# Experts by choice: rows gathered five tiles ahead instead of four, and the late partial sums fetched in one row

## The chip, the cores and the metric

One core of a Trainium2 chip. The metric is the device time of one execution in microseconds; for the kernel before it is the median of three runs. All stages of the model run in one launch on this core.

## The reference

A graph attention layer with a feed-forward block comes first; the change touches only the last stage, a mixture of experts over 4096 rows of 512 values.

```python
K = 2; EPS = 1e-06; B, S, D, F, E = (8, 256, 512, 256, 8)   # here 4096 rows
logits = xf @ router_w
gate_vals, idx = jax.lax.top_k(logits, K)
gates = jax.nn.softmax(gate_vals, axis=-1)
out = jnp.zeros_like(xf)
for e in range(E):
    h = jax.nn.relu(xf @ w1[e] + b1[e]) @ w2[e] + b2[e]
    y = _layernorm(xf + h, gamma[e], beta[e])
    w = jnp.sum(jnp.where(idx == e, gates, 0.0), axis=-1)
    out = out + w[:, None] * y
```

The result is added to x, and xf is the layer norm of x. Both x and its norm stand side by side in one table in memory.

## The kernel before, in words

The function `experts` first loads all rows once to compute the router's logits, picks each row's two experts, and sorts the rows into tiles of 128 rows that share an expert. Every row occurs once by its first choice and once by its second. For each choice there are EACH = 39 tiles (32 full ones and up to 7 that are not full), so a loop runs over SLOTS = 78 slots. Slots 0 to 38 are the first half (first choices), slots 39 to 77 the second (second choices).

A row of the table `z3` (called t_z in the profile) has WITH_SUM = 1028 values of 4 bytes in two parts of PART = 514: the sum so far, and the normalised row with its two gates. In the first half a slot gathers whole rows of `z3` by an indirect DMA, computes its expert, adds gate times result to the sum part, and scatters the whole rows to the table `summed` (t_summed). In the second half a slot gathers whole rows of `summed` and scatters its result to `out`. So whole rows of the second half can be gathered only when all scatters of the first half have landed. For the first LATE_PARTS slots of the second half (`late(n)`, here slots 39 to 43) this is split: the normalised part comes from `z3` in the gather's turn, and the sum part comes from `summed` later, by `late_part(n)`, with a semaphore of its own, `moved_part`.

All of these DMAs are issued by GpSimd (POOL), in this order and each after its own waits:

```python
for n in range(LEAD):
    gather(n)
for n in range(SLOTS):
    if n + LEAD < SLOTS:
        gather(n + LEAD)
    if n:
        scatter(n - 1)
    if late(n):
        late_part(n)
```

`gather(m)` (L1989 for a late slot's part, L1995 for whole rows) fills ring buffer m modulo TURN = 8; it waits until slot m-8 is done (`e_done`) and, where that was a slot of the first half, until its scatter has landed (`wait_put`). `scatter(n)` (L2015 in the first half, L2012 in the second) waits for `e_done` of slot n. `late_part(n)` (L2005) waits by `all_put` for the landing of the last four scatters of the first half.

In iteration n the other engines do the following, in this order.

- TensorE (PE): `turn_rows(n + 2)` transposes the gathered rows (L2274, after `wait_rows`), then it reads the number of slot n+1's expert from memory into a register (`expert`), then `up(n + 1)` (L2332), `down_bias(n)` (L2346), `down(n)` (L2351) and `turn_hidden(n + 1)` (L2340).
- ScalarE (ACT): `columns(n + 2)` copies the transposed rows (L2059), `hidden(n + 1)` (L2064), `hidden_columns(n + 1)` (L2070), the root of slot n's variance (L2099), which waits for VectorE, and `outer(n + 1)` (L2076).
- VectorE (DVE): `spread(n)` adds the row (L2220; its start is used below as the clock of the loop) and takes the statistics (L2222, L2224), `outer(n - 1)` ends the slot before (L2246, signals `e_done`), then `gain(n)` and `add_base(n)` (L2230). For a late slot `add_base(n)` stands after `gain(n)` and first waits for `moved_part` of that slot.

Of the kernel before, what the change touches and what calls it, by code (L numbers as in the profile page):

```python
# [25 lines left out]
VROW = HEADS * VHEAD  # L26
PART = C + 2
WITH_SUM = 2 * PART
LATE_PARTS = 5
BOTH = C + VROW  # L30
MERGED = (3, 11, 19, 27)
DVE_HEADS = (HEADS - 1, HEADS - 2)
# [1759 lines left out]
def experts(nc, moved, moved_part, count, z3, router, w1, b1, w2, b2, gamma, beta, summed, b2_home, out):  # L1792
# [10 lines left out]
    KC = C // P  # L1803
    T = NODES // P
    E, _, F = w1.shape
    FC = F // P
    TOP = 2
    EACH = T + E - 1
    SLOTS = TOP * EACH
    TURN = 8  # L1810
    LEAD = 4
    Y = 4
    HALF = 4
    LIST_TURNS = 4
# [2 lines left out]
    with ExitStack() as ctx:  # L1817
        def sb(name, shape, dt=F32):
            return ctx.enter_context(nc.sbuf_tensor("m_" + name, shape, dt))

        def ps(name, shape, dt=F32):
            return ctx.enter_context(nc.psum_tensor("m_" + name, shape, dt))
# [56 lines left out]
        put_at = sb("put_at", [P, SLOTS], I32)  # L1879
        part_of = sb("part_of", [P, 2, LATE_PARTS], I32)  # L1880
        turned = [ps(f"turned{b}", [P, C]) for b in range(2)]
# [41 lines left out]
        def second(n):  # L1923
            return n >= EACH

        def late(n):
            return EACH <= n < EACH + LATE_PARTS

# [3 lines left out]
        def wait_put(eng, n):  # L1932
            eng.wait_ge(put[n % Y], count + 16 * (n // Y + 1))
# [5 lines left out]
        @block.sync  # L1939
        def _(eng):  # L1940
            eng.dma_start(router_sb[:, :, :], router.rearrange("(k p) e -> p k e", p=P)).then_inc(s_c, 16)
            eng.dma_start(b2_rows[:, :], b2).then_inc(s_b2_rows, 16)
            z_of = z3[:, PART:PART + C]
            for i in range(T // TURN):
                for u in range(TURN):
                    if i:
                        r_turn.wait(eng, i - 1, u)
                    eng.dma_start(z_rows[:, u, :], tile_rows(z_of, i, TURN, u)).then_inc(r_load.sem(u), 16)
            eng.wait_ge(s_b2_cut, 3 * PARTS - 4)
            eng.dma_start(b2_home, b2_parts[:, :, :]).then_inc(s_b2_home, 16)  # L1950
            eng.dma_start(b1_sb[:, :, :], b1).then_inc(s_w1, 16)
            eng.dma_start(w1_sb[:, :, :, :], w1.rearrange("e (k p) f -> p e k f", p=P)).then_inc(s_w1, 16)
            eng.dma_start(w2_sb[:, :, :, :], w2.rearrange("e (k p) c -> p e k c", p=P)).then_inc(s_w2, 16)
            eng.wait_ge(s_b2_home, 16)
            eng.dma_start(b2_sb[:, :, :], b2_home.rearrange("e k c -> k e c")).then_inc(s_b2, 16)
            for dst, a, landed in ((gamma_sb, gamma, s_gamma), (beta_sb, beta, s_beta)):
                eng.dma_start(flat(dst[:, :, :]), a.rearrange("e c -> (e c)").partition_broadcast(P)).then_inc(landed, 16)

        @block.gpsimd
        def _(eng):  # L1960
            for a, value in ((ones, 1.0), (zeros, 0.0), (eps, EPS), (ones_b, 1.0)):
                eng.memset(a[:, :], value).then_inc(s_cut, 1)
            eng.memset(go_on[:, :, :], 1.0).then_inc(s_cut, 1)
            eng.memset(go_on_e[:, :, :], 1.0).then_inc(s_cut, 1)
            for a, step, n, down, first_one in ((falling, -1, E, 0, E), (row_id, 0, 1, 1, 1), (slot_at, 1, EACH, 0, 0),
                                                (turn_b, 1, T, 0, 0)):
                eng.iota(a[:, :], pattern=[[step, n]], base=first_one, channel_multiplier=down,
                         allow_small_or_imprecise_dtypes=True).then_inc(s_cut, 1)
            eng.iota(iota_2[:, :, :], pattern=[[1, P], [0, 2]], base=0, channel_multiplier=0,
                     allow_small_or_imprecise_dtypes=True).then_inc(s_cut, 1)  # L1970
            eng.wait_ge(s_cut, 11)
            eng.memset(go_on[:, :, 0:1], 0.0).then_inc(s_cut, 1)
            eng.memset(go_on_e[:, :, 0:1], 0.0).then_inc(s_cut, 1)
            for m, of, op, other in ((ident, ones, ALU.is_equal, 0.0), (not_after, zeros, ALU.is_gt, -1.0)):
                eng.affine_select(out=m[:, :], in_=of[:, :], compare_op=op, fill=other, base=0,
                                  pattern=[[1, P]], channel_multiplier=-1).then_inc(s_cut, 1)

            z3_parts, summed_parts = (a.rearrange("n (h w) -> (n h) w", h=2) for a in (z3, summed))

            def gather(n):  # L1980
                u = n % TURN
                if n >= TURN:
                    e_done.wait(eng, 0, n - TURN)
                    if not second(n - TURN):
                        wait_put(eng, n - TURN)
                if late(n):
                    if n == EACH:
                        eng.wait_ge(s_ready, 2)
                    eng.indirect_dma_start(rows_sb[:, u, PART:], None, z3_parts,  # L1989
                                           bass.IndirectOffsetOnAxis(part_of[:, 1, n - EACH:n - EACH + 1], 0)  # L1990
                                           ).then_inc(got[u], 16)
                else:
                    if second(n):
                        all_put(n)
                    eng.indirect_dma_start(rows_sb[:, u, :], None, summed if second(n) else z3,  # L1995
                                           bass.IndirectOffsetOnAxis(row_of[:, n:n + 1], 0)).then_inc(got[u], 16)

            def all_put(n):
                if n <= EACH + LATE_PARTS:
                    for k in range(EACH - Y, EACH):  # L2000
                        wait_put(eng, k)

            def late_part(n):
                all_put(n)
                eng.indirect_dma_start(rows_sb[:, n % TURN, 0:PART], None, summed_parts,  # L2005
                                       bass.IndirectOffsetOnAxis(part_of[:, 0, n - EACH:n - EACH + 1], 0)
                                       ).then_inc(moved_part[n - EACH], 16)

            def scatter(n):
                e_done.wait(eng, 0, n)  # L2010
                if second(n):
                    eng.indirect_dma_start(out, bass.IndirectOffsetOnAxis(put_at[:, n:n + 1], 0), y[:, n % Y, :], None,  # L2012
                                           bounds_check=NODES - 1, oob_is_err=False).then_inc(put[n % Y], 16)
                else:
                    eng.indirect_dma_start(summed, bass.IndirectOffsetOnAxis(put_at[:, n:n + 1], 0), rows_sb[:, n % TURN, :], None,  # L2015
                                           bounds_check=NODES - 1, oob_is_err=False).then_inc(put[n % Y], 16)

            eng.wait_ge(s_ready, 1)
            eng.wait_ge(s_gate_home, 16)
# [4 lines that stand above are left out]
                    gather(n + LEAD)  # L2024
                if n:
                    scatter(n - 1)
                if late(n):
                    late_part(n)
            scatter(SLOTS - 1)
            for n in range(SLOTS - Y, SLOTS):  # L2030
                wait_put(eng, n)
# [72 lines left out]
        def _(eng):  # L2104
# [69 lines left out]
            for c in range(TOP):  # L2174
# [33 lines left out]
                if c == 1:  # L2208
                    few = token[:, c, 0:LATE_PARTS]
                    st.link(nc.vector.tensor_scalar(part_of[:, 0, :], few, 2.0, None, ALU.mult))  # L2210
# [167 lines left out]
def graph_layer(nc, a, out):  # L2378
# [5 lines left out]
    with ExitStack() as ctx:  # L2384
        moved = [ctx.enter_context(nc.semaphore(f"moved{n}")) for n in range(MOVES)]
        moved_both = [ctx.enter_context(nc.semaphore(f"moved_both{n}")) for n in range(2)]
        moved_part = [ctx.enter_context(nc.semaphore(f"moved_part{n}")) for n in range(LATE_PARTS)]
        stages(nc, a, out, moved, moved_both, moved_part, scratch)
# [58 lines left out]
```

## Time and profile before

| | |
|---|---|
| median of three runs | 3304.93 us (3302.91 to 3306.12) |
| profiled execution, its own time | 3307.92 us |
| span of its profile | 3306.2 us |
| PE, PEld, DVE, ACT, POOL busy | 2772.7, 1710.6, 2521.6, 1701.4, 1935.0 us |
| mean granted clock | 0.93 of full speed |
| the 78 slots in that span | from about 2868 to 3297 us |

The span is the time between the first and the last instruction that the profiler saw; the execution's own time is 1.7 us longer. The busy shares are those of the whole program; the loop over the slots is its last eighth and has limits of its own.

### The profile page before, as it was taken

The page shows a single profiled execution, that of the slowest core. Times are in us where ns is not written, and L with a number is a line of the kernel's source. Part 1 is how long each engine was busy: PE and PEld are TensorE (multiplying, and loading weights), DVE is VectorE, ACT ScalarE, POOL GpSimd, SP SyncE. Part 2 cuts the span into 40 slices and gives each one's busy share as a digit, 9 for nine tenths or more (in the row PEclk, how much of TensorE's full clock was granted, in tenths as well). Part 3 has the DMA queues.
Part 4 walks back from the last instruction along what each step waited for, and adds up shares of the span by engine and source line. Part 5 has one row for each costly group of instructions (what it writes and reads, how often), then busy time and mean ns, then how long its engine had stood idle before and what let it go on. Part 6 is the DMA issues. An engine that isn't in the chain of part 4 may idle for free. (4 is left out here: it accounts for less than half of the span.)

```text
span 3306.2 us, 51862 instructions
## 1 busy us (share of the span) xinstructions
PE 2772.7 (84%) x12057; PEld 1710.6 (52%) x12057; DVE 2521.6 (76%) x5238; ACT 1701.4 (51%) x5713; POOL 1935.0 (59%) x1959
## 2 busy tenths in 40 slices
PE   6987888780888888886999999998999997699797
PEld 6544444450333333332555655567888885355454
DVE  8776666660999999998999999996566563577576
ACT  5222222220666566555999999993443432244343
POOL 2777777776777777776777777762222221044344
PEclk9888888885999999998999999997999999899999
DMA  4554555544888888887777878774221222765343
GB/s 168 197 182 167 173 173 170 174 147 152 261 258 261 262 260 259 261 258 243 216 231 231 233 231 232 230 205 112 68 71 61 74 71 94 226 200 188 119 155 108
DMA packets 248065, 610.11 MB, mean 185 GB/s; under 512 B 60466, under 2 KB 69578, under 8 KB 243037
## 3 DMA queue, kind: packets, MB, share of 16 engines
q0 software_dynamic: 130000, 376.49, 38.2%
q1 hardware_dynamic: 113661, 230.27, 20.2%
q8 instruction: 113, 1.85, 0.2%
q14 instruction: 179, 1.47, 0.1%
q10 hardware_dynamic: 4112, 0.03, 0.1%
HBM read 488.89 MB, written 123.26 MB: 185 GB/s over the span
## 5 line engine op out<-in xcount | busy, mean ns | idle before, releaser
L1275 PE MATMUL at_pair<-wide,hot_t 128*128 x1152 | 583.2, 621 | 120.7 <-ACT hot_t L1126 106.4
L1324 PE MATMUL at_pair<-product,v_hot 128*128 128x260 f32 x2304 | 617.2, 400 | 48.7 <-DVE product L1074 21.2
L364 POOL DMA_INDIRECT records<-staged,address x544 | 545.6, 1003 | 182.5 <-issue 161.9
L914 POOL DMA_INDIRECT fetched<-t_v,at_index x504 | 487.3, 967 | 188.0 <-issue 86.6
L904 POOL DMA_INDIRECT fetched<-t_k,at_index x504 | 487.4, 967 | 154.8 <-issue 102.0
L1324 PEld LDWEIGHTS at_pair<-product,v_hot 128*128 128x128 f32 x2304 | 394.5, 190 | 266.2 <-issue 158.4
L660 PE MATMUL qkv_prod<-wide 128*128 128x512 f32 x768 | 397.5, 681 | 96.8 <-ACT wide L404 96.8
L1066 DVE TENSOR_TENSOR wide<-at_pair,wide 128x520 f32 x576 | 397.3, 690 | 14.1 <-issue 10.3
L1275 PEld LDWEIGHTS at_pair<-wide,hot_t 128*128 128x128 f32 x1152 | 186.2, 189 | 385.0 <-issue 381.8
L1134 ACT ACTIVATE product<-product 128x64 f32<-128x64 f32 x864 | 215.9, 250 | 286.3 <-DVE product L993 284.9
L993 DVE TENSOR_TENSOR product<-at_pair,fetched 128x512 f32<-128x512 f32 x504 | 342.3, 682 | 25.3 <-DMA fetched<-t_k,at_index 18.9
L947 DVE TENSOR_REDUCE raw_score<-product 128x7 f32<-128x448 f32 x576 | 329.7, 575 | 0.0
L660 PEld LDWEIGHTS qkv_prod<-wide 128*128 128x128 f32 x768 | 165.6, 220 | 304.5 <-issue 205.6
L1213 ACT ACTIVATE product<-fetched,act_weight 128x65 f32<-128x65 f32 x1008 | 288.8, 333 | 0.0
L1074 DVE TENSOR_TENSOR product<-fetched,at_turn 128x390 f32<-128x390 f32 x504 | 276.4, 549 | 2.7 <-ACT act_weight L1193 1.5
L1526 POOL TENSOR_TENSOR f_base<-f_base,wide 128x512 f32<-128x512 f32 x32 | 41.0, 1280 | 343.6 <-DVE f_rows_in L1567 343.6
L1168 ACT ACTIVATE at_shared<-iota_f,low_neg 128x128 f32<-128x128 f32 x576 | 222.7, 387 | 0.0
L1718 PE MATMUL f_up<-f_zT,f_w 128*128 128x256 f32 x1536 | 192.5, 285 | 17.5 <-ACT f_h L1674 17.5
L1207 ACT ACTIVATE v_hot<-at_shared 128x128 f32<-128x128 f32 x576 | 175.8, 305 | 45.3 <-PE at_pair L1324 42.2
L1718 PEld LDWEIGHTS f_up<-f_zT,f_w 128*128 128x128 f32 x1536 | 186.7, 192 | 20.7 <-ACT f_h L1674 20.6
L1718 PE MATMUL f_down<-f_w,f_hT 128*128 128x512 f32 x768 | 185.6, 397 | 2.3 <-issue 2.3
L392 ACT COPY staged<-bias_sb 128x128 f32<-128x128 f32 x34 | 10.1, 297 | 333.2 <-DMA records<-staged,address 332.2
(327 smaller groups left out, 4647.7 us busy)
## 6 DMA issues: line engine op xcount, KB each, us to landing
row_bc<-in_src SPq DMA_DIRECT2D x34, 1024.0 KB, 5.4
pair_rows<-kept_v SPq DMA_DIRECT2D x72, 260.0 KB, 4.2
low_bc<-low_row SPq DMA_DIRECT2D x34, 512.0 KB
wide<-in_x SPq DMA_DIRECT2D x64, 256.0 KB, 3.2
t_z<-wide SPq DMA_DIRECT2D x64, 256.0 KB, 3.1
kept_v<-pair_rows SPq DMA_DIRECT2D x36, 260.0 KB, 3.7
kept_v<-at_shared SPq DMA_DIRECT2D x36, 260.0 KB, 3.8
records<-staged,address POOLq DMA_INDIRECT x544, 2.3
```

Of the source, the lines that this page charges most:

```text
L364: eng.indirect_dma_start(records, bass.IndirectOffsetOnAxis(address[:, b, u:u + 1], 0), staged[:, b, u, :], None,).then_inc(put[b][u], 16)
L660: last = nc.tensor.matmul(prod[n][:, :], zT[:, c, kc * P:(kc + 1) * P], w[:, n, kc, :], start=(kc == 0), stop=(kc == KC - 1))
L904: eng.indirect_dma_start(fetched[:, n % SLOTS, 0:C], None, k, bass.IndirectOffsetOnAxis(index[:, t:t + 1], 0)).then_inc(s_row[n % SLOTS], 16)
L914: eng.indirect_dma_start(fetched[:, n % SLOTS, :], None, v, bass.IndirectOffsetOnAxis(index[:, t:t + 1], 0)).then_inc(s_row[n % SLOTS], 16)
L947: nc.vector.tensor_reduce(raw[:, b, u % PAIR, u // PAIR, 0:heads], product[:, u % 4, 0:heads * D].rearrange("p (h d) -> p h d", d=D), AX.X ...
L993: nc.vector.tensor_tensor(product[:, u % 4, 0:C], q_edge[u % 4], key_rows(i, u), ALU.mult).then_inc(r_product.sem(u), 1)
L1066: nc.vector.tensor_tensor(to, pair[u % 3][:, :, 0:HALF], to, ALU.add).then_inc(r_total.sem(u), 1)
L1074: nc.vector.tensor_tensor(product[:, u % 4, 0:V_DVE * VHEAD].rearrange("p (h w) -> p h w", h=V_DVE), value_rows(m, u)[:, 0:V_DVE * VHEAD]. ...
L1213: ins = nc.scalar.activation(product[:, u % 4, h * VHEAD:(h + 1) * VHEAD], value_rows(m, u)[:, h * VHEAD:(h + 1) * VHEAD], ACT.Copy, scale ...
L1275: nc.tensor.matmul(q_edge[u % 4], hot_t[:, g % 2, u % BATCH * P:(u % BATCH + 1) * P], q_sb[:, bass.ds(at, 1), :].rearrange("p a c -> p (a ...
L1324: last = nc.tensor.matmul(pair[u % 3][:, n, 0:HALF], hot[:, u % 4, :], product[:, u % 4, n * HALF:(n + 1) * HALF], start=True, stop=True)
L1718: last = nc.tensor.matmul(out, stationary(a, k), moving(b, k), start=(k == 0 and n == 0), stop=(k == chunks - 1 and n == len(PASSES) - 1))
```

## The change

`LEAD` goes from 4 to 5: five gathers are issued ahead of the loop, and in iteration n the gather of slot n+5. `LATE_PARTS` goes from 5 to 6: slot 44, whose gather now comes before the last scatter of the first half, also takes its two parts separately, and there is one more `moved_part` semaphore and one more column in `part_of`. And the sum parts of the late slots are no longer fetched one in each iteration: in iteration 39, after `scatter(38)`, all six are issued in a row.

```diff
-LATE_PARTS = 5
+LATE_PARTS = 6
...
-    LEAD = 4
+    LEAD = 5
...
                     gather(n + LEAD)
                 if n:
                     scatter(n - 1)
-                if late(n):
-                    late_part(n)
+                if n == EACH:
+                    for m in range(LATE_PARTS):
+                        late_part(EACH + m)
             scatter(SLOTS - 1)
```

## Rows read from the trace of the kernel before

**Rows 1.** The page: busy time by engine, share of the span, instructions.
```profile
PE 2772.7 (84%) x12057; PEld 1710.6 (52%) x12057; DVE 2521.6 (76%) x5238; ACT 1701.4 (51%) x5713; POOL 1935.0 (59%) x1959
```

**Rows 2.** Stretches: start:end, length; busy PE, PEld, DVE, ACT, POOL; clock, DMA, GB/s.
```profile
2868.00:3084.00 216.00, 198.91 (x795) 121.66 (x794) 145.03 (x325) 94.99 (x245) 94.75 (x82) 0.97 0.54 179
3084.00:3140.00 56.00, 39.94 (x128) 23.26 (x127) 25.46 (x56) 15.77 (x42) 20.20 (x20) 0.88 0.36 113
3140.00:3284.00 144.00, 140.91 (x559) 85.72 (x558) 106.34 (x234) 66.66 (x176) 66.12 (x56) 1.00 0.46 150
```

**Rows 3.** Timeline of VectorE, L2220, slots 0, 36, 39, 40, 44, 45, 46, 75.
```profile
2885.38 0.69 DVE L2220 TENSOR_TENSOR m_y<-m_down,m_rows 128x512 f32<-128x512 f32 x1 [13.76 <-PE m_down L2351]
...
3069.66 0.69 DVE L2220 TENSOR_TENSOR m_y<-m_down,m_rows 128x512 f32<-128x512 f32 x1 [2.77 <-PE m_down L2351]
...
3083.51 0.69 DVE L2220 TENSOR_TENSOR m_y<-m_down,m_rows 128x512 f32<-128x512 f32 x1 [0.80 <-PE m_down L2351]
3093.72 0.69 DVE L2220 TENSOR_TENSOR m_y<-m_down,m_rows 128x512 f32<-128x512 f32 x1
...
3130.05 0.69 DVE L2220 TENSOR_TENSOR m_y<-m_down,m_rows 128x512 f32<-128x512 f32 x1
3133.93 0.69 DVE L2220 TENSOR_TENSOR m_y<-m_down,m_rows 128x512 f32<-128x512 f32 x1
3140.43 0.69 DVE L2220 TENSOR_TENSOR m_y<-m_down,m_rows 128x512 f32<-128x512 f32 x1 [2.68 <-PE m_down L2351]
...
3283.02 0.69 DVE L2220 TENSOR_TENSOR m_y<-m_down,m_rows 128x512 f32<-128x512 f32 x1 [1.28 <-PE m_down L2351]
```

**Rows 4.** Timeline of one late gather, slot 11's: start, us, engine, line, [idle before].
```profile
2918.70 1.43 POOL L2015 DMA_INDIRECT t_summed<-m_rows,m_put_at  x1 [2.29 <-DVE m_rows L2246]
...
2920.44 0.97 POOL L1995 DMA_INDIRECT m_rows<-t_z,m_row_of  x1 [0.30 <-issue]
...
2925.53 0.66 PE L2274 MATMUL m_turned<-m_ident,m_rows 128*128 128x128 f32 x4 [0.30 <-DMA m_rows<-t_z,m_row_of]
...
2926.99 1.99 PE L2332 MATMUL m_up<-m_w,m_zT 128*128 x8 [0.80 <-issue]
```

**Rows 5.** Waits from 2900 to 3084 us: total us, times, longest.
```profile
PE m_up L2332 <- issue: 6.8, 14, 0.8
...
PE m_turned L2274 <- DMA m_rows<-t_z,m_row_of: 4.5, 7, 1.1
```

**Rows 6.** Waits from 3140 to 3290 us: total us, times, longest.
```profile
PE m_turned L2274 <- DMA m_rows<-t_summed,m_row_of: 1.3, 1, 1.3
```

**Rows 7.** L1995, the gathers issued from 2880 to 3086 us (33): to landing.
```profile
DMA to landing us min/median/max: 4.3/5.0/5.6
```

**Rows 8.** L1995, the gathers issued from 3135 to 3306 us (29): to landing.
```profile
DMA to landing us min/median/max: 4.1/4.2/4.5
```

**Rows 9.** L2015, the first half's 39 scatters: to landing.
```profile
DMA to landing us min/median/max: 3.6/3.8/3.9
```

**Rows 10.** DMA issues from 2868 to 2900 us: six gathers in a row, then two; median.
```profile
m_rows<-t_z,m_row_of POOLq DMA_INDIRECT x8, 5.7
```

**Rows 11.** Timeline of GpSimd where the second half begins.
```profile
3086.73 1.01 POOL L2015 DMA_INDIRECT t_summed<-m_rows,m_put_at  x1 [1.93 <-DVE m_rows L2246]
3089.62 0.98 POOL L2005 DMA_INDIRECT m_rows<-t_summed,m_part_of  x1 [1.88 <-DMA t_summed<-m_rows,m_put_at]
3090.90 0.94 POOL L1995 DMA_INDIRECT m_rows<-t_summed,m_row_of  x1 [0.30 <-issue]
```

**Rows 12.** Timeline of VectorE and TensorE in the same stretch.
```profile
3092.97 0.69 DVE L2230 TENSOR_TENSOR m_z_cols<-m_rows,m_z_cols 128x512 f32<-128x512 f32 x1 [6.26 <-DMA m_rows<-t_summed,m_part_of]
...
3097.20 0.44 PE L2340 MATMUL m_h_turned<-m_ident,m_h 128*128 128x128 f32 x2 [4.57 <-ACT m_h L2064]
...
3098.22 3.40 PE L2332 MATMUL m_up<-m_w,m_zT 128*128 x8
...
3101.86 1.98 PE L2351 MATMUL m_down<-m_w,m_hT 128*128 x4
```

## The prediction

> **What bounds the kernel now.** I read the page first: PE is the busiest engine [rows 1]. Those are shares of the whole program. The change touches only the loop over 78 slots, so I asked for the busy times of its stretches. PE is busy 92% of the first half, 71% where the halves meet, and 98% of the rest of the second [rows 2]. PE sets the pace, and the question is what keeps it idle.
>
> The clock that I use is the start of the row addition on VectorE, once per slot; y(n) is that of slot n. From y(36) to y(39) three rounds take 13.85 us, 4.617 each: this is the round when nothing is late. The first half takes 198.13 us for 39 rounds, where 39 times 4.617 is 180.06: 18.07 too much. From y(39) to y(46), seven rounds take 56.92 instead of 32.32. From y(46) to y(75), 29 rounds take 142.59 instead of 133.89: 8.70 too much [rows 3]. These three excesses are what the change can win.
>
> Then I asked the timeline why a round is long. In the first half a gather lands late: slot 11's is issued at 2920.44, right behind the scatter of slot 5, and TensorE starts on its rows at 2925.53, after waiting for them. The wait itself is 0.30, but the up product then starts 0.80 late as well, with nothing named [rows 4]. In the program the read of the expert's number stands behind the wait for rows, so it can't run ahead while the queue is held; I take that for the 0.80. A gather then has to land up to about 0.8 before the transposes want it. Added up, 4.5 us of waits for rows and 6.8 of such unnamed idle stand in the first half [rows 5].
>
> The place of a gather in the round can be computed. A scatter is issued 3.22 after y: y(39) at 3083.51, scatter of slot 38 at 3086.73 [rows 3, 11]. The gather behind it comes 1.74 later [rows 4]. With four ahead, gather(m) stands behind scatter(m-6), so it is issued at y(m-5) + 4.96. TensorE wants it when it has finished slot m-3, at about y(m-3), two rounds after y(m-5): 9.23. That leaves 4.27 us to land. The first half's gathers take 4.3 to 5.6 [rows 7], the second half's 4.1 to 4.5 [rows 8]. So every gather of the first half is a little late and every one of the second on the edge, which fits the two excesses, 0.46 a round and 0.30 a round.
>
> Where the halves meet, VectorE waits 6.26 for the sum part of slot 39; meanwhile ACT stands at its root, and PE at ACT's copy, 4.57 [rows 12]. The next four rounds are as long: y(40) to y(44) takes 36.33 us, 9.08 each [rows 3]. Each goes in a circle: the late part of slot n is issued only behind scatter(n-1), which waits for slot n-1, whose end waits for its own late part. From y to the scatter 3.2, to the late part behind it 1.3, to its landing 3.4, and the addition ahead of the next y, 0.7, make 8.6 of it [rows 11, 12].
>
> **The change, part by part.**
>
> *Lead of five, first half.* Gather(m) stands behind scatter(m-7), at y(m-6) + 4.96; TensorE wants it at y(m-6) + 13.85. That leaves 8.89 us. The longest landing, 5.6 [rows 7], and the register read of 0.8 [rows 4] are 6.4. All waits for rows go: -18.07. More can't, since 4.617 is PE's own work; the other end is that only what carries a named wait goes (rival 1). What is late next? The buffer. Gather(m) needs the landing of scatter(m-8), issued a round, 4.62 us, before scatter(m-7); the gather comes up 1.74 behind the latter, so 6.36 us are there for a landing of 3.6 to 3.9 [rows 9]. It doesn't wait. The gather ahead of the loop becomes a seventh issued in a row; it is wanted some four rounds later.
>
> *Lead of five, second half.* The same shift for gathers of 4.1 to 4.5 us [rows 8], whose buffers wait for no scatter's landing: -8.70 from y(46) to y(75). After y(75) nothing is gathered: 0.
>
> *The late parts in a row.* The first wait stays: the scatter of slot 38 must land, part 39 is issued at 3089.62 on the old time scale, and y(40) comes at 3093.72 [rows 3, 11]. GpSimd's next five go 1.28 apart [rows 11]: 3090.90 to 3096.02. The part of slot 40 is there by about 3094.3, and VectorE asks for it 0.7 ahead of y(41). VectorE is not held any more: its own round is 3.88, from y(44) to y(45) [rows 3], so y(41) is at 3097.6. For y(42) TensorE does a round after its 4.57 idle; its up product takes 3.40 there [rows 12] instead of 1.99 [rows 4], because the granted clock has fallen to 1.2 GHz, and its down product ends at 3103.8 [rows 12]. So y(42) is at 3103.8, and from there rounds of 4.617 give y(46) at 3122.3, instead of 3140.43 [rows 3]: -18.1.
>
> Behind the six parts in GpSimd's queue stand gather(45), now at 3097.3, and the scatter of slot 39, at 3098.6, some 1.2 later than before. That scatter releases nothing soon: its buffer is used again at slot 43. Gather(45) is wanted at y(42), 3103.8, less 0.8: 5.7 us are left, and gathers in a row take 5.7 [rows 10]. It fits with nothing to spare; missing it costs 1 us at most. Cheapest case: the clock doesn't fall, 1.4 to 2 more won. Dearest: one more round at the low clock (y(45) to y(46), 6.50, is 1.88 above a round [rows 3]), 1 for gather(45), and 1 for a part 39 that shares the DMA engines: 4 less.
>
> The Trainium skill (page "SBUF — State Buffer", section "SBUF: two separate sides") has a rule against a long row of issues on GpSimd: while VectorE runs an operation that takes the port both share, GpSimd can't write its descriptors. The trace leans its way for scatters: 1.43 us beside a busy VectorE, 1.01 with VectorE idle [rows 4, 11]. By that rule six issues would end 2.5 us later and gather(45) with them, and the gain of this part would be 15.6 instead of 18.1.
>
> *The rest.* Slot 44 takes two gathers instead of one, 1.28 of GpSimd's time, which idles 1.9 in a round [rows 11]; without that cover it would be the 1.28. One more column in two tiny VectorE operations and one more semaphore: 0.
>
> **The sum.** -18.07 - 18.1 - 8.70 = -44.9 us. On the profiled execution: span 3306.2 to 3261.3, its own time 3307.92 to 3263.0. The median of the runs was 3304.93, 3.0 lower, so 3260.0: 1.4% less.
>
> **The rivals.**
>
> 1. *Only the named waits are waits for rows.* In the first half 4.5 us are charged to rows, in 7 waits [rows 5], in the second 1.3, in one [rows 6]; each brings up to 0.8 behind it. That is 10.1 and 2.1. If the rest is a cost of PE's own instruction stream, the gain is 10.1 + 18.1 + 2.1 = 30.3: 3275. For it: half of the up products that start late follow no named wait (14 against 7 [rows 5]). Against: 4.27 us of room and landings of 4.1 to 5.6 give just such delays, and clean rounds of 4.617 stand between them.
>
> 2. *The seam gives back half.* Six parts and a gather share the DMA engines, and the clock stays low for some rounds: 9 of the 18.1 are lost, 3269. For it: gather(45) has no room. Against: each term above is small, and the DMA engines are 36% busy in this stretch [rows 2]. The Trainium skill says that DMAs of any engine end up on the same 16 DMA engines and interleave ("DMA: Bandwidth & Descriptors", section "Issuing engines are not separate DMA queues"), so a row of parts could stretch the first, the only one that VectorE stands at; no row here shows by how much.
>
> 3. *Slower: the buffer takes the place of the lead.* If a scatter landed X us after its issue and X were long, GpSimd would stand in gather(m) until scatter(m-8) + X and issue scatter(m-6) 1.3 behind it, so two rounds would take X + 1.3. That reaches 4.617 a round at X = 7.9, the old 5.08 at 8.9, and the whole 44.9 is eaten at 1.15 a round, X = 10.2; at 10.5 the kernel would take 3310. Landings are 3.9 at most [rows 9].
>
> 4. *No change.* Another engine binds at the old pace. VectorE's round of 3.88 against 4.617 [rows 3] and the clean rounds speak against it: 3305.
>
> **Chances.** The forecast 0.66, rival 1 0.14, rival 2 0.12, rival 3 0.03, rival 4 0.02, and 0.03 for something between 3276 and 3298. The forecast's own range is 3257 (clock kept, and a microsecond) to 3266 (4 less, and 2 of small waits). For 8 in 10 the range takes in rival 2 and reaches to rival 1: 3255 to 3274. A measurement of this kernel tells about 0.2%, 6.6 us, from no change. Faster 0.95, same 0.02, slower 0.03.
>
> **What the profile after would show.** Rounds of 4.617 from y(0) to y(39) and from y(46) to y(75), no transposes that wait for rows, and no idle ahead of the up product; if idle of 0.2 to 0.8 stays there without a late row, rival 1. GpSimd's gathers 1.7 behind a scatter; a longer gap is the wait of rival 3. At the seam one wait of about 6.3 on VectorE, y(41) 3.9 after y(40), y(42) 6.2 after that, then rounds of 4.6, and L2005 six times, 1.28 apart. The prediction is wrong if y(39) to y(46) takes more than 43 us instead of 38.8, or if the rounds of the first half stay above 4.7 on average.

## The result, and the profile after

| | before | after |
|---|---|---|
| median of four runs | 3305.52 us (3302.91 to 3309.45) | 3263.76 us (3258.89 to 3266.38) |
| ratio | | 0.9871, interval 0.9854 to 0.9888 |
| profiled execution, its own time | 3307.92 us | 3266.38 us |

41.8 us are gone, where 44.9 were forecast; 3260.0 was the number. In a second measurement the medians were 3312.0 (nine runs) and 3266.84 (four), 45.2 apart, with a ratio of 0.9865 (0.985 to 0.988).

The page of the kernel after, busy time by engine:

```profile
PE 2749.4 (84%) x12057; PEld 1706.2 (52%) x12057; DVE 2523.1 (77%) x5238; ACT 1701.2 (52%) x5713; POOL 1940.2 (59%) x1960
```

This says next to nothing: GpSimd has one instruction more (the second gather of slot 44), and the shares are those of before [rows 1]. The stretches do say something. Kernel after: start:end, length; busy PE, PEld, DVE, ACT, POOL; clock, DMA, GB/s:

```profile
2868.00:3064.00 196.00, 188.55 (x787) 119.10 (x785) 142.88 (x320) 92.76 (x241) 94.02 (x81) 0.96 0.60 197
3064.00:3100.00 36.00, 31.27 (x120) 19.85 (x120) 22.76 (x51) 14.07 (x38) 20.80 (x19) 0.91 0.49 146
3100.00:3242.00 142.00, 142.00 (x584) 88.82 (x583) 111.92 (x247) 70.22 (x186) 70.00 (x59) 1.00 0.49 157
```

PE was busy for 92%, 71% and 98% of the three stretches [rows 2]; now it is for 96%, 87% and 100%. Next, the clock of the loop, the row addition on VectorE, for slots 0, 39, 40, 41, 42, 43, 46, 75 and 77 (L2221 is the old L2220):

```profile
2888.07 0.69 DVE L2221 TENSOR_TENSOR m_y<-m_down,m_rows 128x512 f32<-128x512 f32 x1 [15.27 <-PE m_down L2352]
...
3068.04 0.69 DVE L2221 TENSOR_TENSOR m_y<-m_down,m_rows 128x512 f32<-128x512 f32 x1 [0.80 <-PE m_down L2352]
3078.41 0.69 DVE L2221 TENSOR_TENSOR m_y<-m_down,m_rows 128x512 f32<-128x512 f32 x1
3082.49 0.69 DVE L2221 TENSOR_TENSOR m_y<-m_down,m_rows 128x512 f32<-128x512 f32 x1
3089.16 0.69 DVE L2221 TENSOR_TENSOR m_y<-m_down,m_rows 128x512 f32<-128x512 f32 x1 [2.87 <-PE m_down L2352]
3093.77 0.69 DVE L2221 TENSOR_TENSOR m_y<-m_down,m_rows 128x512 f32<-128x512 f32 x1 [0.79 <-PE m_down L2352]
...
3107.61 0.69 DVE L2221 TENSOR_TENSOR m_y<-m_down,m_rows 128x512 f32<-128x512 f32 x1 [0.78 <-PE m_down L2352]
...
3241.47 0.69 DVE L2221 TENSOR_TENSOR m_y<-m_down,m_rows 128x512 f32<-128x512 f32 x1 [0.80 <-PE m_down L2352]
...
3249.52 0.69 DVE L2221 TENSOR_TENSOR m_y<-m_down,m_rows 128x512 f32<-128x512 f32 x1
```

Differences of these rows, and of the same ones before [rows 3]; y(77) stood at 3291.07 there, 405.69 after y(0):

| us | before | after | change | forecast |
|---|---|---|---|---|
| y(0) to y(39) | 198.13 | 179.97 | -18.16 | -18.07 |
| y(39) to y(46) | 56.92 | 39.57 | -17.35 | -18.1 |
| y(46) to y(75) | 142.59 | 133.86 | -8.73 | -8.70 |
| y(0) to y(77) | 405.69 | 361.45 | -44.24 | -44.9 |
| start of the span to y(0) | 2885.38 | 2888.07 | +2.69 | 0 |

The waits of the kernel after from 2900 to 3064 us, three of its five largest: total us, times, longest.

```profile
POOL t_summed L2015 <- DVE m_rows L2247: 40.9, 21, 2.3
...
POOL t_summed L2015 <- DMA t_summed<-m_rows,m_put_at: 28.4, 15, 1.9
DVE m_y L2221 <- PE m_down L2352: 28.0, 36, 0.8
```

Two entries of before have gone altogether: transposes that wait for rows (4.5 us, 7 times) and an up product that starts late with nothing named (6.8, 14 times) [rows 5]. VectorE waits 0.8 for the down product in each of 36 rounds: PE sets the pace and nothing holds PE. The second line names the landing of a scatter, but by the program a scatter waits for VectorE alone; the landing of the scatter before it only falls at about the same moment, a round of 4.62 later. The seam's own rows on GpSimd, kernel after:

```profile
3071.27 1.01 POOL L2015 DMA_INDIRECT t_summed<-m_rows,m_put_at  x1 [1.93 <-DVE m_rows L2247]
3074.18 0.98 POOL L2005 DMA_INDIRECT m_rows<-t_summed,m_part_of  x1 [1.90 <-DMA t_summed<-m_rows,m_put_at]
3075.47 0.95 POOL L2005 DMA_INDIRECT m_rows<-t_summed,m_part_of  x1 [0.30 <-issue]
...
3080.73 1.27 POOL L2005 DMA_INDIRECT m_rows<-t_summed,m_part_of  x1 [0.30 <-issue]
3082.30 1.09 POOL L1995 DMA_INDIRECT m_rows<-t_summed,m_row_of  x1 [0.30 <-issue]
```

and on VectorE and TensorE:

```profile
3077.66 0.69 DVE L2231 TENSOR_TENSOR m_z_cols<-m_rows,m_z_cols 128x512 f32<-128x512 f32 x1 [6.41 <-DMA m_rows<-t_summed,m_part_of]
...
3081.90 0.69 PE L2341 MATMUL m_h_turned<-m_ident,m_h 128*128 128x128 f32 x2 [4.73 <-ACT m_h L2065]
...
3083.23 3.60 PE L2333 MATMUL m_up<-m_w,m_zT 128*128 x8
...
3089.11 0.60 PE L2275 MATMUL m_turned<-m_ident,m_rows 128*128 128x128 f32 x4
```

There is one wait for a sum part, 6.41, where before there was one per late slot. It costs what it did before [rows 12]: all behind it idles too, and the up product that follows is slow (3.60, with a granted clock of 0.54 from 3083 to 3087 us; from 3087 on it is 1.00 again).

### The profile page after: what moved, and what is told of

It reads as the page before. It is cut to its first block and busy times, and to the rows that moved or that the text cites. A ratio compares the mean times of both kernels' runs of the same rounds, so it can differ in the third digit from the quotient of the medians.

```text
span 3264.6 us, 51866 instructions
## 1 busy us (share of the span) xinstructions
PE 2749.4 (84%) x12057; PEld 1706.2 (52%) x12057; DVE 2523.1 (77%) x5238; ACT 1701.2 (52%) x5713; POOL 1940.2 (59%) x1960
```

## The experiments

In the first group of runs (lead only, row only, read first, lead of six) the stages ahead of the loop took about 600 to 640 us longer on that chip, for the kernel before as well: y(0) is at 3489.61, 3523.59, 3525.38 and 3524.29 in these four traces. The rounds of the loop are as on the other chips, so I compare distances between row additions, and give ratios to the kernel before on the same chip.

**The lead alone.** The kernel before with `LEAD = 5` and, since slot 44 is then gathered too early for whole rows, `LATE_PARTS = 6`; the parts stay one in each iteration.

```diff
-LATE_PARTS = 5
+LATE_PARTS = 6
...
-    LEAD = 4
+    LEAD = 5
```

> Five ahead and six late slots, but each sum part fetched in its own iteration, as before. By my theory the waits for rows go in both halves (18.1 and 8.7 us) and the circle at the seam stays, for one slot more: y(39) to y(47) about 66 us where the kernel before has 61.5, so the whole is 22 us faster than before, about 3283. If only the waits that carry a name were waits for rows (rival 1), the halves give back 12 and the whole is 8 faster, about 3297.

Measured: y(0) to y(39) 179.97, as in the kernel after; y(39) to y(47) 65.88 (before 61.53), y(47) to y(75) 129.23; the loop 383.14, 22.55 less. Ratio 0.994 (0.9922 to 0.9959). Its GpSimd timeline at the seam shows the circle, one part in each round of about 9:

```profile
3675.72 0.98 POOL L2005 DMA_INDIRECT m_rows<-t_summed,m_part_of  x1 [1.90 <-DMA t_summed<-m_rows,m_put_at]
3677.01 0.94 POOL L1995 DMA_INDIRECT m_rows<-t_summed,m_row_of  x1 [0.30 <-issue]
3683.59 1.03 POOL L2012 DMA_INDIRECT out<-m_y,m_put_at  x1 [5.65 <-DVE m_y L2246]
3684.92 0.98 POOL L2005 DMA_INDIRECT m_rows<-t_summed,m_part_of  x1 [0.30 <-issue]
```

The second part stands behind a scatter that waits over 5 us for its slot, and that slot waits for its own part. All this came as expected (66 for y(39) to y(47), 22 less for the whole). So the lead by itself wins both halves, and makes the seam dearer by the 4.3 us that one more slot in the circle costs.

**The row alone.** The kernel before, its five late parts in a row, lead still four.

```diff
-                if late(n):
-                    late_part(n)
+                if n == EACH:
+                    for m in range(LATE_PARTS):
+                        late_part(EACH + m)
```

> Four ahead and five late slots as before, but the five sum parts in a row. If the two parts of the change only add, this is 18 us faster than before, 3287. By my theory they don't: the whole-row gather of slot 44 now stands behind the five parts in GpSimd's queue, 5.1 us later than before, and TensorE wants it one round earlier than with five ahead; it should cost about 3.5, so 14.6 faster, 3291, and a wait of TensorE's transposes for rows of 3 us or more near y(42) is to be seen.

Measured: 199.25, 44.41 and 145.58. The two halves stay as they were (198.85 and 145.36 in a second trace of the kernel before), the seam wins 12.5, and the loop is 397.29. Ratio 0.9967 (0.9947 to 0.9987). Why not 17.35? Its GpSimd timeline, and y(39) to y(42):

```profile
3728.94 0.98 POOL L2005 DMA_INDIRECT m_rows<-t_summed,m_part_of  x1 [1.87 <-DMA t_summed<-m_rows,m_put_at]
...
3735.44 1.27 POOL L1995 DMA_INDIRECT m_rows<-t_summed,m_row_of  x1 [0.30 <-issue]
```

```profile
3722.84 0.69 DVE L2221 TENSOR_TENSOR m_y<-m_down,m_rows 128x512 f32<-128x512 f32 x1 [0.80 <-PE m_down L2352]
3733.13 0.69 DVE L2221 TENSOR_TENSOR m_y<-m_down,m_rows 128x512 f32<-128x512 f32 x1
3737.21 0.68 DVE L2221 TENSOR_TENSOR m_y<-m_down,m_rows 128x512 f32<-128x512 f32 x1
3748.05 0.69 DVE L2221 TENSOR_TENSOR m_y<-m_down,m_rows 128x512 f32<-128x512 f32 x1 [7.04 <-PE m_down L2352]
```

and TensorE:

```profile
3741.15 1.12 PE L2275 MATMUL m_turned<-m_ident,m_rows 128*128 128x128 f32 x4 [3.85 <-DMA m_rows<-t_summed,m_row_of]
```

With four ahead the gather behind the parts is gather(44), and it is issued 12.60 after y(39). TensorE waits 3.85 for its rows, the wait of 3 us or more that was expected (the gain is 12.5 for 14.6), and y(42) comes 10.84 after y(41) instead of 6.67. In the kernel after gather(44)'s rows are on the way before the seam, and gather(45) stands there, wanted a round later. The two edits need each other: the lead's -22.55 and the row's -12.5 at the seam (the halves differ by no more than two traces of the kernel before do) make -35, together they make -44.2. Of the 9.2 between, 4.35 is the sixth slot in the circle, which the row takes away, and 4.85 is this late gather, which the lead takes away.

**The register read moved ahead.** The kernel before, with the read of the expert's number ahead of the transposes. This parts the forecast (the read held behind the wait for rows is the unnamed 0.80) from rival 1 (a cost of PE's own stream, which no move would touch).

```diff
+                if n + 1 < SLOTS:
+                    e = expert(eng, n + 1)
                 if n + 2 < SLOTS:
                     turn_rows(n + 2)
                 if n + 1 < SLOTS:
-                    e = expert(eng, n + 1)
                     up(n + 1, e)
```

> The kernel before with one thing moved: TensorE reads the number of the next expert ahead of its wait for rows instead of behind it. If the unnamed idle ahead of the up products (6.8 us in the first half) is this read, held up behind the wait, it goes: the second half's 8.7 us of excess go nearly all, since its landings of 4.2 fit in 4.27, and 3 to 6 of the first half's 18.1, where landings of 5.0 still don't fit: 3291 to 3294. If that idle is a cost of the instruction stream (rival 1), nothing changes: 3305.

Measured: 190.17, 57.54 and 142.38, against 198 to 199, 57 and 142.6 to 145.4 before; ratio 0.9974 (0.9953 to 0.9996). I ran it again on a chip where the stages ahead of the loop take as long as in the first measurement, and the kernel before once more.

> The kernel before with the expert's number read ahead of the wait for rows, once more, beside traces of the kernel before from a like machine. First half 198.5 there, 190.2 in the first run of this: 190 again if the read costs 8 us there. From y(46) to y(75) 142.6 to 145.4 there: 142 if the read doesn't set the second half's pace and late landings do, 135 if it does.

> The kernel before once more, for a trace of its loop beside the others of this call: y(0) to y(39) 198 us and y(46) to y(75) 142.6 as in the first trace, each within 1.5 us, if the excesses of the rounds are its own and not one execution's; y(39) to y(46) 56.9.

Measured: read first 191.88, 56.71 and 140.75, loop 397.40, one run of 3302.38 (kernel before there 3307.19, seven runs); kernel before 198.85, 57.49 and 145.36, loop 409.76, one run of 3312.13. The waits of TensorE in the first half, kernel before again:

```profile
PE m_up L2332 <- issue: 7.4, 16, 0.9
...
PE m_turned L2274 <- DMA m_rows<-t_z,m_row_of: 3.5, 7, 0.9
```

and read first again:

```profile
PE m_turned L2274 <- DMA m_rows<-t_z,m_row_of: 6.8, 13, 1.5
```

The unnamed idle is gone, and transposes that wait for rows rise from 7 to 13: what was hidden in the read is now named. By the means of the traces (198.13, 198.85 and 199.25 before, 190.17 and 191.88 with the read first) that gives 7.7 us in the first half, 6 to 9 by which two are compared, where I had expected 3 to 6. In the second half I had expected all 8.7 and got about 3 (142.59, 145.36 and 145.58 before, 142.38 and 140.75 with the read first). The kernel before kept its first half within the 1.5 us that I had expected of a second trace, but not its second, which was 2.8 longer. The waits of the second half say why read first won so little there, kernel before again, 3142 to 3287 us:

```profile
PE m_turned L2274 <- DMA m_rows<-t_summed,m_row_of: 2.8, 3, 1.9
...
PE m_up L2332 <- issue: 2.1, 10, 0.2
```

and read first again, 3137 to 3277 us:

```profile
PE m_turned L2274 <- DMA m_rows<-t_summed,m_row_of: 3.9, 4, 1.8
```

The rows themselves are late there. That was so in the first trace too. The landings of [rows 7] to [rows 10] stand on a few of the transfers only, because the view counts those alone whose semaphore has all its updates in the trace. With the last update that the trace holds for each gather, the 33 of [rows 7] land 4.1 to 6.1 us after their issue (median 4.6), and the 29 of [rows 8] also 4.1 to 6.1 (median 4.4), where the view says 4.1 to 4.5; the one of 6.1 is the gather behind the single named wait of [rows 6].

With these landings each round can be compared with its gather. In both traces of read first every round from y(m-3) to y(m-2) that takes over 4.65 is longer than 4.615 by the time that gather(m) lands after y(m-3), plus 0.13 to 0.16 us (from slot 5 on, the seam left out). In the kernel before the same holds with 0.6 at the least (median 0.62, up to 1.3 where TensorE stands in a named wait; one round has 2.2). So late landings make all of the excess in both halves, and the read behind the wait takes about 0.45 us of room from every gather.

**Six ahead.** The kernel after with one more, to measure the margin that rival 3 lives on.

```diff
-LATE_PARTS = 6
+LATE_PARTS = 7
...
-    LEAD = 5
+    LEAD = 6
```

> Six ahead and seven late slots, parts in a row. The gather of slot m now stands right behind the scatter of slot m-8, whose landing it needs, so GpSimd waits for each landing (3.6 to 3.9 from its issue) before it can issue the gather and the next scatter. By my theory (rival 3 with its condition met) a round of the first half is then a landing plus 1.3, 5.0 to 5.2 instead of 4.62: 15 to 22 us slower than the changed kernel, 3279 to 3286, while the second half, whose buffers need no landing, stays at 4.62. If more lead is simply harmless, 3264.

Measured: 241.89, 51.21 and 133.85, loop 435.21, 73.8 more than with five, and 29.5 more than before; ratio to the kernel before 1.0051 (1.0032 to 1.0071). Its GpSimd timeline in the first half:

```profile
3599.84 1.01 POOL L2015 DMA_INDIRECT t_summed<-m_rows,m_put_at  x1 [0.30 <-issue]
3605.12 1.23 POOL L1995 DMA_INDIRECT m_rows<-t_z,m_row_of  x1 [4.27 <-DMA t_summed<-m_rows,m_put_at]
3606.65 1.01 POOL L2015 DMA_INDIRECT t_summed<-m_rows,m_put_at  x1 [0.31 <-issue]
3611.69 1.20 POOL L1995 DMA_INDIRECT m_rows<-t_z,m_row_of  x1 [4.03 <-DMA t_summed<-m_rows,m_put_at]
```

and its TensorE there, two rounds on:

```profile
3603.07 0.66 PE L2275 MATMUL m_turned<-m_ident,m_rows 128*128 128x128 f32 x4 [1.20 <-DMA m_rows<-t_z,m_row_of]
...
3609.64 0.66 PE L2275 MATMUL m_turned<-m_ident,m_rows 128*128 128x128 f32 x4 [1.22 <-DMA m_rows<-t_z,m_row_of]
```

With six ahead gather(m) waits for the scatter just before it. It comes 5.28 and 5.04 after that scatter's issue (3599.84 to 3605.12, 3606.65 to 3611.69), and the next scatter 1.53 behind the gather, so a round is about 6.6 us there (3605.12 to 3611.69; 6.20 on average over the first half). This is rival 3, shown. Of the 73.8 us, 61.9 are lost in the first half and 11.6 at the seam: GpSimd is so far behind that the scatter of slot 38 is issued 12.9 after y(39) instead of 3.2. The second half keeps its pace.

My expectation was 15 to 22 us, from a landing of 3.6 to 3.9 [rows 9] and rounds of 5.0 to 5.2. Two things were missing. The gather starts 0.75 us after the last update of the scatter's semaphore, in every round of this trace; a landing does not release at once. And the landing itself comes later: a median of 4.4 us after the issue for slots 0 to 31, up to 6.2, where it is 3.8 in the kernel before. There GpSimd had idled ahead of a scatter (2.29 ahead of slot 5's [rows 4]), while these are issued 0.30 behind a gather of 128 whole rows. Scatters of slots 32 to 35, issued 0.30 behind gathers of half rows in this trace, land after 3.5 to 3.6. That the bytes just ahead delay the scatter fits this, but no run varies them alone.

The last scatters of the half say nothing of it. Those of slots 37 and 38 land after 2.1 to 2.5 us in every trace of the kernels before and after, and in the kernel before at most one packet of a whole row's size moves while one of them is under way: these tiles seem to have next to no rows to write. So it is no contrast that the part at 3074.18 in the kernel after comes 2.91 behind the scatter it waits for; with six ahead slot 37's is as quick, 0.30 behind a gather too (2.98):

```profile
3774.79 1.01 POOL L2015 DMA_INDIRECT t_summed<-m_rows,m_put_at  x1 [0.30 <-issue]
3777.77 0.98 POOL L1989 DMA_INDIRECT m_rows<-t_z,m_part_of  x1 [1.97 <-DMA t_summed<-m_rows,m_put_at]
```

**After once more**, beside the next three.

> The changed kernel once more: y(0) to y(39) 180.0, y(39) to y(46) 39.6, y(46) to y(75) 133.9, the loop from y(0) to y(77) 361.5 us, 44 less than the kernel before, in whatever time the stages ahead of it take.

Measured: 179.98, 39.41 and 133.85, loop 361.29, y(0) at 2881.43, median 3266.84 (four runs). The loop repeats within 0.2 us.

**What the seam's one wait still costs.** Three kernels, each the one before it with one thing more. First VectorE's and ScalarE's order, so that neither stands at slot 39's part when there is other work: the addition of a late sum moves behind the next slot's row addition, and ScalarE's `outer` behind the next `hidden_columns`.

```diff
                 wait_rows(eng, n)
                 spread(n)
+                if late(n - 1):
+                    add_base(n - 1)
                 if n:
                     outer(n - 1)
                 if not late(n):
                     add_base(n)
                 gain(n, e)
-                if late(n):
-                    add_base(n)
...
-            outer(0, e)
...
+                this = e
                 if n + 2 < SLOTS:
                     columns(n + 2)
                 if n + 1 < SLOTS:
                     hidden(n + 1)
                     e = expert(eng, n + 1)
                     hidden_columns(n + 1, e)
+                outer(n, this)
...
-                if n + 1 < SLOTS:
-                    outer(n + 1, e)
```

> The changed kernel with two things moved to take the one wait that is left at the seam off the path. VectorE adds the base of a late slot behind the row addition of the next slot, and ScalarE prepares that base behind its hidden columns instead of behind the root, so neither stands in front of TensorE's next copy. The first sum part still lands 9.6 us after y(39); the 4.7 idle of TensorE and the fall of its clock should go, and y(41) comes at y(39) + 12.1 instead of 14.5. Then the gather of slot 45, behind six parts in GpSimd's queue, is wanted a round earlier than now and is late by about 3: y(39) to y(46) 36.8 instead of 39.6, the loop 358.7. If GpSimd's queue had room (no such wait), 33.6 and 355.5. If another engine takes up the wait, 39.6.

Measured: 179.98, 40.81 and 133.85, loop 362.68, 1.2 more than after instead of 2.8 less; median 3264.13, ratio 0.9858 (0.9844 to 0.9872). y(41) is 11.88 after y(39), instead of 14.45 in the kernel after, but y(43) then 11.11 after y(42). Its GpSimd row of gather(45), and TensorE:

```profile
3080.01 0.94 POOL L1995 DMA_INDIRECT m_rows<-t_summed,m_row_of  x1 [0.30 <-issue]
```

```profile
3085.18 1.11 PE L2274 MATMUL m_turned<-m_ident,m_rows 128*128 128x128 f32 x4 [4.12 <-DMA m_rows<-t_summed,m_row_of]
3086.09 3.73 PE L2332 MATMUL m_up<-m_w,m_zT 128*128 x8
```

The wait has moved, and the slow up product behind it with it: slot 45's rows are wanted earlier than they can come, being behind six parts. I had expected them 3 us late, and they cost 4.12 and 1.8 more in the up product (3.73 us). So next gather(45) goes between the third and the fourth part:

```diff
+                if n == EACH + 1:
+                    for m in range(LATE_PARTS // 2, LATE_PARTS):
+                        late_part(EACH + m)
                 if n:
                     scatter(n - 1)
                 if n == EACH:
-                    for m in range(LATE_PARTS):
+                    for m in range(LATE_PARTS // 2):
                         late_part(EACH + m)
```

> As the kernel with the deferred base, and the row of six parts is split: three behind the last scatter of the first half, then the whole-row gather of slot 45, then the other three, ahead of the scatter of slot 39. If it is the place of that gather in the queue that costs 3 us in the other, y(39) to y(46) is now 33.6 to 34.5 and the loop 355.5 to 356.5, 5 to 6 below the changed kernel. If the order in the queue doesn't matter, it equals the other.

Measured: 38.65 at the seam, loop 360.53; median 3262.07, ratio 0.9853 (0.984 to 0.9867). That is 0.9 less than after, where 5 to 6 less were expected. The order in the queue matters, but the wait moved on to gather(46):

```profile
3079.82 0.97 POOL L1995 DMA_INDIRECT m_rows<-t_summed,m_row_of  x1 [0.30 <-issue]
```

```profile
3085.50 0.87 PE L2277 MATMUL m_turned<-m_ident,m_rows 128*128 128x128 f32 x4 [2.28 <-DMA m_rows<-t_summed,m_row_of]
```

Last, both gathers behind the first three parts, and six ahead in the rest of the second half, where no buffer waits for a scatter's landing.

```diff
-                if n + LEAD < SLOTS:
-                    gather(n + LEAD)
+                ahead = LEAD + (n > EACH + 1)
+                if n + ahead < SLOTS:
+                    gather(n + ahead)
                 if n == EACH + 1:
+                    gather(n + LEAD + 1)
                     for m in range(LATE_PARTS // 2, LATE_PARTS):
```

> As the kernel with the split row, and behind the first three sum parts both the gathers of slots 45 and 46 are issued, so that the rest of the second half runs six ahead, where a buffer needs no landing. In the split one the gather of slot 46 stood behind three parts and a scatter and was late by 2.3, with the clock falling after it. By my theory that wait goes and nothing else comes: y(43) at y(39) + 20.3 as there, then rounds of 4.617, y(39) to y(46) 34.1 and the loop from y(0) to y(77) 356.0, 5.3 below the changed kernel; the whole 3260 where the changed kernel has 3265. If six ahead costs in the second half what it cost in the first, its rounds go to 5 or more and the loop to over 370.

Measured: 179.98, 34.64 and 133.85, loop 356.52: 4.9 less than after and 49.2 less than before. The median is 3262.6 (four runs), the ratio 0.9859 (0.9842 to 0.9875): as a whole it can't be told from the kernel after, since y(0) is at 2891.12 in its profile. That six ahead costs nothing in the second half is shown too (133.85): a buffer there needs no landing of a scatter. Two of its GpSimd rows, and y(43):

```profile
3081.03 1.18 POOL L1995 DMA_INDIRECT m_rows<-t_summed,m_row_of  x1 [0.30 <-issue]
3082.52 1.20 POOL L1995 DMA_INDIRECT m_rows<-t_summed,m_row_of  x1 [0.30 <-DVE m_y L2251]
```

```profile
3092.75 0.69 DVE L2225 TENSOR_TENSOR m_y<-m_down,m_rows 128x512 f32<-128x512 f32 x1 [1.82 <-DMA out<-m_y,m_put_at]
```

What is late now, 1.82 us, is the landing of slot 39's scatter of results, issued at 3088.01 behind the other three parts; the addition of slot 43 wants its buffer again. Seven rounds at 4.617 are 32.32, so 2.3 are left of the 24.6 that the seam cost before.

## Why the prediction was right

**The clean round.** Taken from three rounds of before, 4.617. The kernel after has 179.97 / 39 = 4.615 and 133.86 / 29 = 4.616. It was PE's own work, as the sum assumed.

**Lead of five, first half.** -18.16 for -18.07. That all the excess came from late rows and the read behind them, and not the named waits alone, is shown by read first (named waits double, unnamed idle gone, and every long round explained by its gather's landing) and by the kernel after (no such idle at all). The margin that I had put at up to 0.8 measures 0.6. Rival 1 had 0.14 and falls.

**Lead of five, second half.** -8.73 for -8.70. The size was right and the lead alone brings it (lead only: rounds of 129.23 / 28 = 4.615), but the reasoning was only partly right. I took it for gathers of 4.1 to 4.5 us on the edge of the 4.27 that they had, so that without the read they would fit. By all its gathers the same trace has 4.1 to 6.1, median 4.4: many were late with or without the read, and moving the read wins only about 3. Five ahead leaves 8.89, more than any of them took.

**The row of parts.** -17.35 for -18.1: y(40) 0.16 later (10.37 after y(39) for 10.21), y(41) 4.08 after it for 3.88, y(42) 6.67 for 6.2, where the up product took 3.60 for 3.40; then clean rounds. The granted clock did fall after PE's idle of 4.73, as before (0.54 of full speed from 3083 to 3087 us, nearly all at the lower level, 1.2 GHz), and the round after y(42) is already 4.61: it did not stay low. Rival 2 had 0.12 and falls. Its condition, gather(45) without room, was too dark: the gather is issued at 3082.30, lands 5.5 us later and its rows are transposed at 3089.11, 6.8 after the issue and without a wait, so there were 1.3 us to spare. I had counted 0.8 for a read that had no reason to be late here. The 5.7 that I set against it was luck: the view of [rows 10] has landings for two of its eight gathers, and of the six in a row the last three land after 6.6.

On the port that GpSimd and VectorE share: from the first part to the gather behind the sixth it is 8.12 us (3074.18 to 3082.30), where I had counted 7.7. The Trainium skill ("SBUF — State Buffer", section "SBUF: two separate sides") says that GpSimd can't write descriptors while VectorE runs an operation in a mode that takes both of its ports. The trace agrees in direction, with two of the six steps 0.2 to 0.3 longer, and not in size: by the rule I had put it at 2.5. The Trainium skill ("DMA: Bandwidth & Descriptors", section "Issuing engines are not separate DMA queues") also says that DMAs of any engine run on the same 16 DMA engines and interleave. No run here shows a price for it: VectorE's wait for the first part is 6.41 with five more behind it and 6.26 before, but it is 6.41 with the lead alone as well, where no other part is behind it. So none of the 0.15 can be laid to the row.

**The buffer.** The buffer costs nothing in the kernel after, as predicted, but the margin was mis-sized. I set 6.36 us of room against 3.9. The 3.9 came from nine of the 39 scatters [rows 9], and I left out the 0.75 from a landing to the start of what waits for it. In the two traces of the kernel after, full scatters land after a median of 3.8 us and 5.9 at the most, so a gather is free to start after 4.6 as a rule, and after 6.7 at the worst. That worst case happened; in the second trace one gather idles 0.65 instead of 0.30:

```profile
3034.38 0.97 POOL L1995 DMA_INDIRECT m_rows<-t_z,m_row_of  x1 [0.65 <-issue]
```

It is issued 6.66 after its scatter, and costs nothing, as GpSimd idles 1.9 in a round anyway. Rival 3 was one tile away: six ahead costs the loop 73.8 us.

**The whole.** The loop gained 44.24 of the 44.9. Of the 3.4 us that are missing in the profiled execution (3266.38 for 3263.0) 2.7 lie ahead of the loop, where y(0) came 2.69 later, in stages that the change doesn't touch but for one gather in the row ahead of the loop. In the traces at hand y(0) lies from 2881.43 (after, second trace) to 2891.12, and at 2885.38 and 2885.52 for the kernel before: this is scatter between executions, not shown to be a cost of the change. The second measurement's medians are 45.2 us apart.

## What to carry to other kernels

Take the clean round from the stretches where nothing is late; its excess over all rounds is what a change to the waits can win, and named waits are a part of it only, because an instruction queued behind the wait (here a register read) takes its own idle with it. Ask of a landing figure how many of the transfers it stands on: mine stood on two to nine, and hid the late ones. Before gathering further ahead, ask what releases the buffer of that gather: the fifth tile, with the row of parts, made the loop 44 us shorter, and a sixth made it 74 us longer again, by a wait that was not in the trace until then. When one wait ends a stretch, removing it moves it to the next transfer in the same queue: it took three steps (4.12, then 2.28, then 1.82 us) to turn one wait into 4.9 us.

## What the runs showed of the hardware that was not expected

- Scatters issued 0.30 behind a gather of 128 whole rows landed a median of 4.4 us after their issue, 3.8 where GpSimd had idled some 2 to 3 us ahead of them, and 3.5 to 3.6 behind gathers of half rows.
- The instruction that waits for a scatter's landing started 0.75 us after the last update of its semaphore.
- Gathers of the same size in one trace of the kernel before landed 4.1 to 6.1 us after their issue, and 6.6 when they were the fourth to sixth issued in a row.
- A register read behind the wait for rows cost TensorE up to 0.9 us in a round: rows had to land 0.6 us ahead of their time instead of 0.15. Over 39 rounds that was 6 to 9 us.
- On one chip the stages ahead of the loop took some 600 us longer, with a mean granted clock of 0.855 for 0.93, and the loop's clean rounds were the same to 0.01 us.
